# Four graph layers on one Trainium2 core: column-split count matmuls, a last layer in two float16 parts, and neighbour codes stored as byte pairs

## The chip, the cores and the metric

The kernel runs as one program on one core of a Trainium2 chip. The metric is the device time of one execution in microseconds (us); lower is better.

## The reference

`x` is 4096 x 64 and `adj` is 4096 x 4096, sparse, symmetric in where it is non-zero. Each layer normalizes `x`, applies a ReLU and adds the layer's result to `x`.

```python
h = jnp.maximum(_layernorm(x), 0.0); x = x + relu((adj @ h) @ W0.T + b0)              # layer 0
h = jnp.maximum(_layernorm(x), 0.0); x = x + lorentz_attention(h, adj)                # layer 1
h = jnp.maximum(_layernorm(x), 0.0); x = x + expmap0((w @ logmap(h_i, h_j)) @ W2 + b2)# layer 2
h = jnp.maximum(_layernorm(x), 0.0)                                                   # layer 3:
support = h @ W3
mask = (adj != 0)
rank = jnp.cumsum(mask, axis=1); deg = rank[:, -1:]
k = jnp.minimum(deg, 100.0)
pos = rank - (deg - k)
w = mask * jnp.where(pos > 0, 0.5 ** (k - pos), 0.0)
x = x + w @ support + b3
```

A weight of layer 3 is thus a power of two whose exponent is the number of neighbours that follow in the row.

## The kernel before, in words

Five instruction streams (SyncE issues loads, TensorE, VectorE, ScalarE, GpSimd) run in orders written out by hand and meet at semaphores. Node features lie as 32 tiles (T) of 128 nodes by 64 columns.

**Layer 0** takes 64 steps (2 halves of the output nodes x 32 tiles, from the last tile to the first). A step loads a 128 x 2048 tile of the transposed matrix into a ring of eight. VectorE makes its 0/1 mask in bfloat16 (`mask0`, L1543; a ring of four) and adds the tile to the running degree sums (`degree0`, L1549). TensorE (`tile0`) multiplies the tile by the features (4 matmuls of 64 columns, float32, two records each in the trace) and then, in `counts`, the mask by two constant 128 x 128 triangles, `tri_rest` for the tile before and `tri_above` for this one: 8 matmuls of 128 weight columns and 512 moving columns. They accumulate in PSUM the exponent of each weight of layer 3. ScalarE (`make_code`, L1102) turns the 128 x 2048 counts into bytes in two calls, `made[:, k, u * UNIT:(u + 1) * UNIT]`, and stores them in DRAM. `mask0` of step s waits for the counts of step s-3; `counts` waits for the mask and for the codes of the step before. After the last step VectorE copies the sums (`sums_out0_v`, L1472), TensorE applies the weights (`to_nodes`, L580) and VectorE updates X (`update0`, L1515).

**Layers 1 and 2** read the matrix twice more. Layer 1's step has 16 matmuls of 64 columns in float16 (`scores`, L746) and 4 in float32 (`gather1`).

**Layer 3** takes 64 steps again (`step3`). Its tiles come in three groups (GROUPS: tiles 0-7, 8-15, 16-31), because their features are ready in that order: steps 0-15, 16-31 and 32-63. For each step SyncE loads one 128 x 2048 code tile (a ring of 16), and `power(q)` turns code into weight by multiplying it by 128 and writing it as a 16-bit integer, whose bits are the bfloat16 power of two: ScalarE does columns 0-1023 (L1390) and VectorE columns 1024-2047 (L2042). Sixteen weight tiles can wait; `power(q)` for q >= 16 waits for step q-16. TensorE multiplies them by the features, which are cut into three bfloat16 parts (`S3`): 12 matmuls a step. Between the steps the streams carry the end of layer 2 and the features of layer 3 for groups 1 and 2 (`last_passage3`). For group 2 that is: `nodes2(2)` (TensorE, L969) at q 3, `tangent_...` (VectorE, L1883 on) at q 10, `to_tangent(2)` (L888) at q 8 and `weighted(2)` (L898) at q 10 of TensorE, `z_out`, `v_square` (ScalarE, L1055), `length` to `feats3` (VectorE, L1903 to L1963, q 20 to 26) with two roots and a square on ScalarE, `to_last(2)` and `weighted_last(2)` (TensorE, q 25 and 27), then `part_a`, `rest_a`, `part_b`, `rest_b` (L1055, L2148, L1055, L1972), which cut the parts; only then may step 32 start. GpSimd adds the bias to X (L558) once the last parts are made. After step 63 the sums are copied out, turned (L580) and added to X (L2165).

Of the kernel before, what the change touches and what calls it, by code (L numbers as in the profile page):

```python
# [15 lines left out]
I16 = mybir.dt.int16  # L16
ALU = mybir.AluOpType
# [4 lines left out]
D = 64  # L22
P = 128
# [111 lines left out]
W_SCALE = 2.0 ** (127 - MAX_NEIGH)  # L135


def graph_layers(nc, x, adj_t, codes, w0_t, b0, w1_t, b1, wq_t, bq, wk_t, bk, scalars, w2, b2, w3, b3, out):
    ctx = ExitStack()
    with ctx:  # L140
# [46 lines left out]
        trest = sb("trest", [P, TG])  # L187
        tri_above = sb("tri_above", [P, P], BF16)
# [111 lines left out]
        def S3(a, b, k):  # L300
            at = a // TG * HALF
            v = TB[:, at:at + 3 * HALF // 4].bitcast(BF16).rearrange("p (t s c) -> p t s c", t=TG, s=3)
            return v[:, a % TG:a % TG + b - a, k, :]

# [40 lines left out]
        def _(sp):  # L345
# [83 lines left out]
            for q in range(2 * T):  # L429
# [5 lines left out]
                if q >= CODES:  # L435
                    sp.wait_ge(sem("pw_ready_a"), q - CODES + 1)
                    sp.wait_ge(sem("pw_ready_v"), q - CODES + 1)
# [9 lines left out]
        def _(pool):  # L447
# [106 lines left out]
            for g in range(G):  # L554

                pool.wait_ge(sem("parts3_ready"), len(GROUPS))
# [6 lines left out]
        def _(pe):  # L563
# [236 lines left out]
            for s in range(2 * T):  # L800
# [7 lines left out]
                if s == 13:  # L808
                    pe.wait_ge(sem("qhh_out"), 2)
                    fold_low(1, 2)  # L810
                if s == 2 * T - 1:
                    break
# [101 lines left out]
            def weighted_last(q):  # L914
                pe.wait_ge(sem("turned_out"), 2 * q + 2)
                through(q, wbd["w3"][:, :], None)
# [134 lines left out]
        def _(act):  # L1051
# [45 lines left out]
            def make_code(h, s, k, at, stored):  # L1097
                for u in range(2):
# [3 lines left out]
                    nc.scalar.activation(made[:, k, u * UNIT:(u + 1) * UNIT], PS[:, (4 + 2 * u) * BANK:(6 + 2 * u) * BANK],  # L1102
# [179 lines left out]
            def z_out(q, k, scale=1.0, last=False):  # L1282
                one("z_out", part(cen, q), linear_out(q, last), ACT.Copy, ("through", k), scale=scale)
# [9 lines left out]

            def part_b(q):
                one("part_b", S3(*GROUPS[q], 1), part(cen, q), ACT.Copy, ("rest_a", q + 1))
# [8 lines left out]
            def last_passage2(n):  # L1304
# [15 lines left out]
                if n == 53:  # L1320
                    z_out(0, 2, W_SCALE)
                    part_a(0, 2)
                if n == 54:
                    part_b(0)
# [20 lines left out]
            def last_passage3(q):  # L1345
# [8 lines left out]
                if q == 10:  # L1354
                    z_out(1, 4, W_SCALE, True)
                    part_a(1, 4)
                if q == 12:
                    part_b(1)
# [13 lines left out]
                if q == 30:  # L1372
                    one("part_a", S3(*GROUPS[2], 0), linear_out(2), ACT.Copy, ("through", 6), scale=W_SCALE)
                if q == 31:
                    part_b(2)
                if q == 56:
                    one("sums_out3_a", TA[:, 0:UNIT], PS[:, 4 * BANK:6 * BANK], ACT.Copy, ("agg3_done", 48))

            def power(q):
# [10 lines left out]
                nc.scalar.activation(pw(q)[:, 0:UNIT].bitcast(I16), code(q)[:, 0:UNIT], ACT.Copy, scale=BF_STEP)\  # L1390
# [5 lines left out]
            one("sums_out3_a", TA[:, UNIT:UNIT + BANK], banks(6, 7), ACT.Copy, ("agg3_done", 2 * T))  # L1396
# [3 lines left out]
        def _(dve):  # L1400
# [422 lines left out]
            for s in range(2 * T):  # L1823
# [12 lines left out]
                if s == 14:  # L1836
                    copy_out("qll_out_v", q_ll[:, HALF:N], banks(2, 4).bitcast(F16), ("qll_ready", 2))
                if s >= T:
# [127 lines left out]
            def rest_a(q):  # L1966
                dve.wait_ge(sem("part_a"), q + 1)
                V.tensor_tensor(part(cen, q), part(cen, q), S3(*GROUPS[q], 0), ALU.subtract).then_inc(sem("rest_a"), 1)

            def rest_b(q):  # L1970
                dve.wait_ge(sem("part_b"), q + 1)
# [231 lines left out]
```

## Time and profile before

| | us |
|---|---|
| median of 3 runs (1071.85 to 1075.57) | 1072.16 |
| the profiled execution | 1072.81 |
| its span, first to last instruction | 1071.1 |

The span is what the trace shows; 1.7 us of the profiled execution lie around it. Busy shares of the span: TensorE 95%, VectorE 81%, ScalarE 72%, GpSimd 24%. Rows that are merged stretch from their first start to their last end; the idle time in brackets is named with what ended it. A matmul's time overlaps the next one's, so the cost of a block is read from start to start.

### The profile page before, as it was taken

Reading aid. Unit: us, or ns where it says so; the run is one execution under the profiler, and the core shown is the slowest. Engines: PE = TensorE matmul, PEld = TensorE weight load, DVE = VectorE, ACT = ScalarE, POOL = GpSimd, SP = SyncE. Lnnn points to the kernel's source line nnn. Section 1 sums busy time; section 2 is a strip of 40 time slices with the busy share of each in tenths; the row PEclk is TensorE's granted clock in tenths of the full one; section 3 lists DMA queues with packets and bytes.
Section 4 is the critical chain, followed back from the end, with each engine's and each line's share of the span. In section 5 each row is a group of like instructions: output and inputs, shape, how many; then the busy total and the mean of one; then the engine's idle time right before and its main releaser. Section 6 shows DMA issues by size and latency. Waiting matters only on the chain.

```text
span 1071.1 us, 15810 instructions
## 1 busy us (share of the span) xinstructions
PE 1019.4 (95%) x5903; PEld 466.1 (44%) x5922; DVE 865.8 (81%) x1012; ACT 769.7 (72%) x808; POOL 251.7 (24%) x140
## 2 busy tenths in 40 slices
PE   6999999999799999999979998999999998989998
PEld 1333333336644444335434443444544554436544
DVE  6999989997677766797679977787789887897781
ACT  4555545554577666786798899888888889997682
POOL 1079000000001000012035554443334334430010
PEclk9999999999989999999989999999999999999999
DMA  9989998992058899788745336556545535446441
GB/s 329 418 319 423 377 352 296 343 396 97 1 184 285 291 307 309 244 281 275 253 141 183 123 114 197 183 171 195 159 158 187 166 119 177 138 158 205 140 168 40
DMA packets 96346, 238.39 MB, mean 223 GB/s; under 512 B 16400, under 2 KB 45072, under 8 KB 79888
## 3 DMA queue, kind: packets, MB, share of 16 engines
q1 hardware_dynamic: 87056, 220.62, 60.4%
q10 hardware_dynamic: 9216, 16.78, 4.1%
q8 instruction: 47, 0.77, 0.3%
q14 instruction: 27, 0.22, 0.1%
HBM read 219.55 MB, written 17.83 MB: 222 GB/s over the span
## 4 chain that ended last, share of the span: by engine, by line
PE 73%; DVE 11%; ACT 9%; issue 5%; POOL 1%; DMA 1%; SPq 0%; DVEq 0%; ACTq 0%; POOLq 0%
PE PS L568 50%; PE PS L746 9%; PE PS L882 4%; PE PS L851 4%; DVE work L2059 2%; ACT work L1252 2%; ACT work L1260 2%; DVE work L2047 2%; DVE ring L2065 1%; ACT work L1263 1%; DVE work L2053 1%; DVE work L1719 1%; PE PS L580 1%; PE PS L602 1%; ACT work L1246 1%
## 5 line engine op out<-in xcount | busy, mean ns | idle before, releaser
L1102 ACT ACTIVATE work<-PS 128x1024 uint8<-128x1024 f32 x128 | 124.0, 1021 | 106.9 <-PE PS L568 105.1
L1719 DVE TENSOR_TENSOR work<-work,ring 128x1024 f32<-128x1024 f32 x128 | 153.0, 1235 | 59.1 <-ACT work L1177 58.9
L1177 ACT ACTIVATE work<-PS,att_sc 128x1024 f32<-128x1024 f32 x128 | 148.1, 1202 | 68.1 <-PE PS L746 59.1
L568 PE MATMUL PS<-ring,work 128*65 128x256 f32 (+1 forms) x600 | 190.6, 465 | 3.8 <-DVE work L2086 3.8
L546 POOL TENSOR_TENSOR ring<-work,ring 128x1024 f32<-128x1024 f32 x57 | 135.3, 2375 | 232.2 <-DVE work L2059 232.2
L568 PE MATMUL PS<-work 128*64 128x512 f32 (+2 forms) x800 | 151.4, 519 | 1.4 <-ACT work L1246 1.2
L2053 DVE SCALAR_TENSOR_TENSOR work<-PS,work 128x1024 f32<-128x1024 f32 x72 | 88.1, 1223 | 55.1 <-PE PS L568 46.6
L746 PE MATMUL PS<-work 128*64 128x512 f16 x1024 | 124.0, 385 | 3.0 <-ACT work L1177 1.6
L568 PEld LDWEIGHTS PS<-ring,work 128*65 128x65 f32 x600 | 80.6, 138 | 90.8 <-issue 65.5
L1252 ACT ACTIVATE work<-work 128x1024 f32<-128x1024 f32 x72 | 76.0, 1055 | 34.2 <-DVE work L2047 34.1
L746 PEld LDWEIGHTS PS<-work 128*64 128x64 f16 x1024 | 59.0, 111 | 79.4 <-issue 34.7
L2059 DVE SCALAR_TENSOR_TENSOR work<-work 128x1024 f32<-128x1024 f32 x72 | 87.9, 1221 | 2.7 <-ACT work L1267 2.1
L568 PEld LDWEIGHTS PS<-work 128*64 128x64 f32 (+2 forms) x800 | 42.8, 120 | 106.9 <-issue 83.8
L1267 ACT ACTIVATE work<-work 128x1024 f32<-128x1024 f32 x72 | 75.9, 1054 | 9.5 <-DVE work L2053 7.1
L851 PE MATMUL PS<-TB,TA 64*128 64x512 f32 x288 | 81.3, 641 | 1.3 <-DVE work L2053 1.3
L568 PE MATMUL PS<-work,TB 128*64 128x512 bf16 x672 | 76.4, 384 | 2.1 <-DVE work L2042 2.1
L1260 ACT ACTIVATE work<-work 128x1024 f32<-128x1024 f32 x72 | 76.2, 1058 | 2.3
L882 PE MATMUL PS<-ident,work 128*128 128x128 f32 x448 | 62.0, 282 | 14.5 <-DVE work L2059 13.6
L1263 ACT ACTIVATE work<-work 128x1024 f32<-128x1024 f32 x72 | 75.1, 1043 | 0.0
L1549 DVE TENSOR_TENSOR TB<-TB,work 128x2048 f32<-128x2048 f32 x32 | 74.9, 2339 | 0.1
L1246 ACT ACTIVATE work<-PS 128x1024 f32<-128x1024 f32 x72 | 72.6, 1009 | 2.3 <-PE PS L568 2.2
L568 PE MATMUL PS<-work,tri_above 128*128 128x512 bf16 x247 | 73.9, 379 | 0.4
(269 smaller groups left out, 1409.9 us busy)
## 6 DMA issues: line engine op xcount, KB each, us to landing
ring<-in_adj_t SPq DMA_DIRECT2D x96, 1024.0 KB, 5.4
ring<-in_adj_t SPq DMA_DIRECT2D x104, 512.0 KB, 4.1
work<-in_adj_t SPq DMA_DIRECT2D x32, 1024.0 KB, 8.1
codes<-work ACTq DMA_DIRECT2D x64, 256.0 KB, 7.1
ring<-codes SPq DMA_DIRECT2D x64, 256.0 KB, 3.8
H<-in_adj_t SPq DMA_DIRECT2D x24, 512.0 KB, 4.3
X<-in_x SPq DMA_DIRECT2D x2, 256.0 KB, 5.3
X<-in_x SPq DMA_DIRECT2D x1, 512.0 KB, 10.7
```

Source lines behind the costliest of these rows:

```text
L546: nc.gpsimd.tensor_tensor(near(n), sums(n), near(n), ALU.mult).then_inc(sem("near_ready"), 1)
L568: return mm(out_ap, lhsT, rhs, start=starts, stop=True, skip_group_check=True)
L746: ins = mm(o[half_rows(e), :], k_hl[:, jt * P + e * D:jt * P + (e + 1) * D], qs[:, i0:i0 + BANK], start=first, stop=not first)
L851: mm(z_banks(n)[:, q * BANK:(q + 1) * BANK], TA[half_rows(q), p * P:(p + 1) * P], TB[half_rows(q), S * STRIP:(S + 1) * STRIP], start=True, ...
L882: ins = nc.tensor.transpose(PS[:, c:c + P], sums(n)[:, q * BANK + i * P:q * BANK + (i + 1) * P], ident[:, :])
L1102: nc.scalar.activation(made[:, k, u * UNIT:(u + 1) * UNIT], PS[:, (4 + 2 * u) * BANK:(6 + 2 * u) * BANK], ACT.Relu).then_inc(sem("codes_ma ...
L1177: nc.scalar.activation(att[:, u, :], PS[:, (4 + 2 * u) * BANK:(6 + 2 * u) * BANK], ACT.Sigmoid, bias=att_sc[:, 2:3], scale=att_sc[:, 1:2]) ...
L1252: nc.scalar.activation(lnr[:, n % ROT, :], root[:, n % ROT, :], ACT.Ln).then_inc(sem("lnr_ready"), 1)
L1260: nc.scalar.activation(sums(n), lnr[:, n % ROT, :], ACT.Exp, scale=0.5).then_inc(sem("root_ready"), 1)
L1719: V.tensor_tensor(prob[:, m % 4, :], att[:, u, :], ring[:, s % RING, u * UNIT:(u + 1) * UNIT], ALU.mult)\
L2053: V.scalar_tensor_tensor(sums(n), z_banks(n), 1.0, sums(n), ALU.max, ALU.add)\
L2059: V.scalar_tensor_tensor(sums(n), sums(n), TAU_MAX, lnr[:, n % ROT, :], ALU.min, ALU.mult)\
```

## The change

1. `counts`: each matmul of 128 weight columns becomes two of 64, into the two halves of PSUM's rows, over the same mask.
2. Layer 3's features are cut into two float16 parts and not three bfloat16 ones: 8 matmuls a step, `part_b` and `rest_b` are gone. To fit float16's range W3 is scaled by a power of two, found in layer 1 (one 128 x 128 matmul after step 18, seven small VectorE operations after steps 16 and 20), and taken out at the end: three VectorE operations of the tail become one with that factor, and the copies carry a constant scale.
3. The bytes of columns n and 1024+n are stored beside each other (`made[:, k, u:HALF:2]`). ScalarE's `power` reads 352 pairs (704 bytes, at stride 2). VectorE reads the other 672 pairs as 16-bit words and makes two tiles of weights from them: the low byte with AND and shift left, the high byte with shift right and AND.
4. GpSimd's bias addition waits for VectorE's last `power` and not for the last parts. VectorE's addition of the first half moves from q 62 to behind its last `power`.

```diff
@@ pairs of two parts
-            v = TB[:, at:at + 3 * HALF // 4].bitcast(BF16).rearrange("p (t s c) -> p t s c", t=TG, s=3)
+            v = TB[:, at:at + HALF // 2].bitcast(F16).rearrange("p (t s c) -> p t s c", t=TG, s=2)
@@ gpsimd
-                pool.wait_ge(sem("parts3_ready"), len(GROUPS))
+                pool.wait_ge(sem("pw_ready_v"), 4 * T)
@@ counts
                 for c in range(2):
-                    ins = add(PS[:, (4 + 2 * u + c) * BANK:(5 + 2 * u + c) * BANK], lhsT,
-                              mask[:, k, u * UNIT + c * BANK:u * UNIT + (c + 1) * BANK], starts)
+                    for e in range(2):
+                        ins = add(PS[half_rows(e), (4 + 2 * u + c) * BANK:(5 + 2 * u + c) * BANK], lhsT[:, e * D:(e + 1) * D],
+                                  mask[:, k, u * UNIT + c * BANK:u * UNIT + (c + 1) * BANK], starts)
@@ step3
+                pe.wait_ge(sem("pw_ready_a"), q + 1)
                 for u in range(2):
-                    pe.wait_ge(sem("pw_ready_v" if u else "pw_ready_a"), q + 1)
+                    pe.wait_ge(sem("pw_ready_v"), 2 * q + u + 1)
                     b = 4 + 2 * h + u
-                    for n in range(3):
+                    for n in range(2):
@@ make_code
-                    nc.scalar.activation(made[:, k, u * UNIT:(u + 1) * UNIT], PS[:, (4 + 2 * u) * BANK:(6 + 2 * u) * BANK],
+                    nc.scalar.activation(made[:, k, u:HALF:2], PS[:, (4 + 2 * u) * BANK:(6 + 2 * u) * BANK],
                                          ACT.Relu).then_inc(sem("codes_made"), 1)
@@ scalar power
-                nc.scalar.activation(pw(q)[:, 0:UNIT].bitcast(I16), code(q)[:, 0:UNIT], ACT.Copy, scale=BF_STEP)\
+                both = pw(q).bitcast(I16).rearrange("p (u n) -> p u n", u=2)[:, :, 0:POW_A]
+                nc.scalar.activation(both, code(q).rearrange("p (n u) -> p u n", u=2)[:, :, 0:POW_A], ACT.Copy, scale=BF_STEP)\
                   .then_inc(sem("pw_ready_a"), 1)
@@ vector, layer 1
+                if s == 16:
+                    V.scalar_tensor_tensor(w3_abs, wbd["w3"][:, :], -1.0, wbd["w3"][:, :], ALU.mult, ALU.max)\
+                     .then_inc(sem("w3_done"), 1)
+                if s == 20:
+                    dve.wait_ge(sem("w3_summed"), 1)
+                    link(V.tensor_reduce(w3_top[:, :], PS[:, 2 * BANK:2 * BANK + P], AX.X, ALU.max))
...
@@ vector power
-                V.tensor_scalar(pw(q)[:, UNIT:2 * UNIT].bitcast(I16), code(q)[:, UNIT:2 * UNIT], BF_STEP, None, ALU.mult)\
+                two = code(q).bitcast(U16)[:, POW_A:UNIT]
+                V.tensor_scalar(pw(q)[:, POW_A:UNIT].bitcast(U16), two, 0xFF, BF_SHIFT, ALU.bitwise_and, ALU.logical_shift_left)\
                  .then_inc(sem("pw_ready_v"), 1)
+                V.tensor_scalar(pw(q)[:, UNIT + POW_A:2 * UNIT].bitcast(U16), two, 1, 0xFF << BF_SHIFT, ALU.logical_shift_right,
+                                ALU.bitwise_and).then_inc(sem("pw_ready_v"), 1)
@@ vector last_passage3
                 if q == 29:
                     dve.wait_ge(sem("part_a"), 3)
-                    V.scalar_tensor_tensor(part(cen, 2), linear_out(2), W_SCALE, S3(*GROUPS[2], 0), ALU.mult, ALU.subtract)\
-                     .then_inc(sem("rest_a"), 1)
-                if q == 31:
-                    rest_b(2)
+                    V.tensor_tensor(S3(*GROUPS[2], 1), linear_out(2), S3(*GROUPS[2], 0), ALU.subtract)\
+                     .then_inc(sem("parts3_ready"), 1)
```

## Rows read from the trace of the kernel before

**Rows 1.** Window of layer 0: busy PE, PEld, DVE, ACT, POOL; clock, DMA share, GB/s
```profile
50.00:250.00 200.00, 197.46 (x854) 65.15 (x870) 193.03 (x123) 106.41 (x113) 43.97 (x8) 1.00 0.94 353
```

**Rows 2.** Timeline of TensorE, one step of layer 0
```profile
190.59 1.94 PE L568 MATMUL PS<-work,H 128*64 128x512 f32 x8
192.46 0.60 PE L568 MATMUL PS<-work,tri_rest 128*128 128x512 bf16 x2
...
194.29 1.94 PE L568 MATMUL PS<-ring,H 128*64 128x512 f32 x8
```

**Rows 3.** Timeline of TensorE, steps of layer 1
```profile
348.89 1.89 PE L568 MATMUL PS<-work 128*64 128x512 f32 x8
350.61 1.90 PE L746 MATMUL PS<-work 128*64 128x512 f16 x16
352.34 1.89 PE L568 MATMUL PS<-work 128*64 128x512 f32 x8
```

**Rows 4.** Timeline of VectorE in layer 0: one step, and the end
```profile
65.19 1.22 DVE L1543 TENSOR_SCALAR work<-work 128x2048 bf16<-128x2048 f32 x1
...
68.53 1.22 DVE L1543 TENSOR_SCALAR work<-ring 128x2048 bf16<-128x2048 f32 x1
...
245.95 4.62 DVE L1549 TENSOR_TENSOR TB<-TB,work 128x2048 f32<-128x2048 f32 x2
251.77 1.23 DVE L1472 COPY TA<-PS 128x1024 f32<-128x1024 f32 x1 [1.20 <-PE PS L568]
```

**Rows 5.** Timeline of TensorE: where `to_nodes` begins after layer 0
```profile
254.27 0.38 PE L586 MATMUL PS<-brow,bones 96*128 96x512 bf16 x1
```

**Rows 6.** Groups by line and form: busy us, mean ns, idle us before
```profile
L568 PEld LDWEIGHTS PS<-work,TB 128*64 128x64 bf16 x672 | 37.3, 111 | 38.4 <-DVE work L2042 3.1 <-issue 2.4 <-ACT work L1390 0.8
L1102 ACT ACTIVATE work<-PS 128x1024 uint8<-128x1024 f32 x128 | 124.0, 1021 | 106.9 <-PE PS L568 105.1 <-remote 1.8
L1390 ACT ACTIVATE work<-ring 128x1024 int16<-128x1024 uint8 x56 | 54.6, 1044 | 0.0
L1055 ACT ACTIVATE work<-work 128x512 f32<-128x512 f32 x6 | 3.7, 623 | 3.4 <-DVE work L1483 3.2
L1472 DVE COPY work<-PS 128x1024 bf16<-128x1024 bf16 x2 | 1.4, 685 | 0.0
```

**Rows 7.** Timeline of TensorE in layer 3
```profile
964.59 3.79 PE L969 MATMUL PS<-ident,work 65*128 65x65 f32 x32
...
978.40 1.09 PE L888 MATMUL PS<-ident,work 128*128 128x128 f32 x8
...
1005.76 1.09 PE L888 MATMUL PS<-ident,work 128*128 128x128 f32 x8 [1.69 <-DVE work L1963]
...
1019.65 1.49 PE L568 MATMUL PS<-work,TB 128*64 128x512 bf16 x12 [0.86 <-DVE work L2042]
...
1046.50 2.05 PE L580 MATMUL PS<-ident,TA 128*128 128x128 f32 x16
```

**Rows 8.** Timelines of VectorE and GpSimd in layer 3
```profile
975.07 1.22 DVE L1899 TENSOR_TENSOR work<-work 128x1024 f32<-128x1024 f32 x1
...
986.71 1.22 DVE L1903 TENSOR_REDUCE st<-work 128x16 f32<-128x1024 f32 x1 [1.10 <-ACT work L1055]
...
989.64 0.69 DVE L2042 TENSOR_SCALAR work<-ring 128x1024 int16<-128x1024 uint8 x1
990.85 0.18 DVE L1909 TENSOR_TENSOR st<-st 128x16 f32<-128x16 f32 x1 [0.52 <-ACT st L1302]
...
1016.30 5.52 POOL L558 TENSOR_TENSOR X<-X,bias 128x1024 f32<-128x1024 f32 x2 [59.86 <-DVE TB L1972]
```

**Rows 9.** Timeline of VectorE at the end
```profile
1064.26 0.69 DVE L1472 COPY TA<-PS 128x512 f32<-128x512 f32 x1 [13.24 <-PE PS L568]
```

**Rows 10.** Windows, columns as in the first group: a clock that fell
```profile
550.00:555.00 5.00, 2.29 (x10) 0.95 (x11) 3.45 (x4) 4.97 (x6) 0.83 (x2) 0.74 0.68 215
555.00:560.00 5.00, 5.00 (x14) 2.31 (x14) 4.08 (x7) 3.83 (x5) 1.94 (x1) 0.58 0.00 0
```

More of the change, by code:

```diff
@@ L16 @@
 I16 = mybir.dt.int16
+I32 = mybir.dt.int32
+U16 = mybir.dt.uint16
 ALU = mybir.AluOpType
@@ L810, in _ @@
                     fold_low(1, 2)
+                if s == 18:
+                    pe.wait_ge(sem("qll_out_v"), 1)
+                    pe.wait_ge(sem("w3_done"), 1)
+                    mm(PS[:, 2 * BANK:2 * BANK + P], bones[:, :], w3_abs, start=True, stop=True).then_inc(sem("w3_summed"), 1)
                 if s == 2 * T - 1:
@@ L1280, in turned_out, with z_out @@
                 one("turned_out", TA[:, a * D:b * D], PS[:, bank * BANK:bank * BANK + (b - a) * D], ACT.Copy, ("turned", k))
-            def z_out(q, k, scale=1.0, last=False):
-                one("z_out", part(cen, q), linear_out(q, last), ACT.Copy, ("through", k), scale=scale)
+            def z_out(q, k, last=False):
+                one("z_out", part(cen, q), linear_out(q, last), ACT.Copy, ("through", k))
             def v_square(q, k):
@@ L1354, in last_passage3 @@
                 if q == 10:
-                    z_out(1, 4, W_SCALE, True)
+                    z_out(1, 4, last=True)
                     part_a(1, 4)
-                if q == 12:
-                    part_b(1)
                 if q == 13:
@@ L1372, in last_passage3 @@
                 if q == 30:
-                    one("part_a", S3(*GROUPS[2], 0), linear_out(2), ACT.Copy, ("through", 6), scale=W_SCALE)
-                if q == 31:
-                    part_b(2)
+                    one("part_a", S3(*GROUPS[2], 0), linear_out(2), ACT.Copy, ("through", 6))
                 if q == 56:
-                    one("sums_out3_a", TA[:, 0:UNIT], PS[:, 4 * BANK:6 * BANK], ACT.Copy, ("agg3_done", 48))
+                    one("sums_out3_a", TA[:, 0:UNIT], PS[:, 4 * BANK:6 * BANK], ACT.Copy, ("agg3_done", 48),
+                        scale=W_SCALE / (F16_TOP / LN_TOP))
             def power(q):
@@ L1395, in _ @@
                 power(q)
-            one("sums_out3_a", TA[:, UNIT:UNIT + BANK], banks(6, 7), ACT.Copy, ("agg3_done", 2 * T))
+            one("sums_out3_a", TA[:, UNIT:UNIT + BANK], banks(6, 7), ACT.Copy, ("agg3_done", 2 * T),
+                scale=W_SCALE / (F16_TOP / LN_TOP))
         @block.vector
@@ L2159, in _ @@
                 power(q)
-            copy_out("sums_out3_v", TA[:, UNIT + BANK:2 * UNIT], banks(7, 8), ("agg3_done", 2 * T))
+            dve.wait_ge(sem("agg3_nodes"), 1)
+            dve.wait_ge(sem("bias3_added"), 1)
+            V.scalar_tensor_tensor(grp(X, 0), z_of(0, 0), w3_top[:, 0:1], grp(X, 0), ALU.mult, ALU.add)\
+             .then_inc(sem("result_ready"), 1)
+            dve.wait_ge(sem("agg3_done"), 2 * T)
+            V.tensor_scalar(TA[:, UNIT + BANK:2 * UNIT], banks(7, 8), W_SCALE / (F16_TOP / LN_TOP), None, ALU.mult)\
+             .then_inc(sem("sums_out3_v"), 1)
             dve.wait_ge(sem("bias3_added"), G)
```

46 lines of the change are left out of this document (22 added, 24 removed).

## The prediction

> **What bounds the kernel now.** First the windows of layer 0, then its timelines on TensorE and VectorE, then the timelines of layer 3, with the groups by form for the prices. Between 50 and 250 us TensorE is busy 197.5 of 200 us and VectorE 193.0 [rows 1]: two engines are nearly full, and a gain on the first is worth only what the second leaves. A TensorE step is 3.70 us: 1.87 us of float32 matmuls and 1.83 us of counts [rows 2]. VectorE needs 3.34 us for mask and degrees where it doesn't wait [rows 4]. But it also carries other work here, so its idle time from 50 to 250 us is only 200 - 193.03 = 6.97 us [rows 1]. Layer 1's step is, bar the weights, the new layer-0 step: eight float32 records in 1.72 us and sixteen 64-column ones in 1.73 us, 3.45 in all [rows 3].
>
> In layer 3 the last twelve steps run from the end of the turning at 1046.50 + 2.05 = 1048.55 to 1064.26: 15.7 / 12 = 1.31 us for a step of 12 matmuls [rows 7, 9]. ScalarE's share of a step is 1044 ns [rows 6] and VectorE's 0.69 us [rows 8], each about 0.1 us less from start to start, so TensorE bounds the steps that are ready. Up to step 32, though, the bound is the chain that makes group 2's features: from 964.59 (nodes out of layer 2) to the turn at 1005.76, before which TensorE already stands idle for 1.69 us, and on to step 32 at 1019.65 [rows 7].
>
> **Layer 0.** The counts' streaming doesn't shrink, since two 64-column matmuls run side by side. What goes is the time lost at each change between 128 and 64 columns: 3.70 - 3.45 = 0.25 us a step. 64 steps would give 16.0 us. The Trainium skill, TensorEngine Tiling, Key Properties, says that changing the tiling mode drains TensorE; the 0.25 us of rows 2 against rows 3 agree, and the sum goes by the rows. I don't take 16.0 us, because VectorE's work stays. Its last degree addition ends at 245.95 + 4.62 = 250.57 [rows 4]. With TensorE ahead its 6.97 us of idle time [rows 1] vanish: 243.6. Then it copies the sums, 1.23 us less 0.1 of overlap: 244.75. `to_nodes`, at 254.27 before [rows 5], starts right after, at 244.85: **9.4 us** gained. TensorE by itself would be there at 254.3 - 16 = 238.3, so it now waits for masks. Bounds: 0, if the loss isn't one of columns, and 16.
>
> ScalarE's code calls, 2 x 1021 ns a step, had 106.9 us of idle time before them [rows 6]; I cost the byte stride at nothing, as a call goes element by element. No row has such a stride. The loads follow VectorE's releases; at 1.31 MB (tile and codes) per 3.34 us the demand is 392 GB/s, against 353 GB/s at a DMA share of 0.94 now [rows 1]. This is close, and I take it as hidden by the ring of eight. The Trainium skill, TensorEngine Tiling, Restrictions, says that column tiling switches fast weight load off. A 64-column load takes 111 ns [rows 6]; sixteen are 1.8 us of a step, beside the matmuls as in layer 1, whose 3.45 us contain as many. So the rule costs nothing here.
>
> The W3 scaling is one matmul and seven VectorE operations in layer 1; at most 0.4 us for TensorE (a 512-column step of rows 3 is 0.22), and in VectorE's idle time there, it is rounded away below.
>
> **The price of the new `power`.** ScalarE: 704 elements; between 623 ns for 512 and 1044 ns for 1024 [rows 6] that is 781 ns, 0.69 from start to start. VectorE: two operations on 672 16-bit words. A small operation of 16 elements takes 0.18 us [rows 8]. The byte-to-int16 call does 1024 elements in 0.69 us [rows 8], about two per ns behind that fixed part; a 1024-element float32 copy from PSUM takes 1.23 us [rows 4], one per ns, and the same copy in bfloat16 685 ns [rows 6]. So two doublings are seen apart: one for a single SBUF source (with 8-bit or 32-bit elements), one for 16-bit elements where the first isn't available. Both together give 0.17 + 672/4 ns = 0.34 us, 0.26 from start to start, **0.51 us a step**. One alone gives 0.84, none 1.54. I take both, since neither row shows a reason against the other, and keep 0.84 and 1.54 as cases. By the table of perf modes in the Trainium skill, VectorE: DVE Perf Modes, a 16-bit `tensor_scalar` in SBUF does four elements a cycle. That would be about 0.34 us too; no row here shows that speed, nor the bitwise operations. TensorE: 8 of 12 matmuls, **0.87 us**. That float16 weights against a bfloat16 moving side cost what either does alone is taken from rows 3 and 7, where both kinds run at 0.22 us a pair.
>
> **Layer 3, stations of group 2's chain.** (a) The nodes at 964.59 wait for VectorE's sum, which stands behind powers 1 to 3; these are 0.1 us cheaper each, the wait takes over from two shorter steps: -0.5 us. (b) The tangent sum ends at 976.29 [rows 8] and now at 975.8; TensorE, five steps ahead of the old pace, waits for it instead of coming at 978.40 [rows 7]: -2.5. (c) Two steps stand between the turn and `weighted(2)`: -0.9, so `length` begins at 986.71 - 3.4 = 983.3 [rows 8]. VectorE has rest and ten powers before that, 0.7 + 5.1 us from 975.8: ready at 981.6. (d) From `length` to the features 19.0 us. In it, power 20 and the wait for ScalarE's root behind four powers (0.25 us cheaper each) go from 1.25 us (989.64 to 990.85) to about 0.6, powers 21 and 22 give 0.1 each, the second root 0.3: -1.2. Features at 1005.7 - 4.6 = 1001.1. (e) Then turn 1.1, two steps 1.7, weights 2.05 (sixteen matmuls of the kind at 1046.50), `part_a` 1.04, the one difference left 1.2 (as any 1024 elements that read PSUM): 1008.2. Steps 27 and 28 are done by then, step 29 waits for power 29, which stands behind that difference (0.5), and steps 29 to 31 take 2.6. Step 32 starts at 1011.3 and not at 1019.65: **8.3 us**. (f) From 1019.65 to 1064.26 were 44.6 us: 32 steps, 2.05 for turning, and stalls while GpSimd's bias addition slowed VectorE. New: 32 x 0.87 + 2.05 = 29.9: **14.7 us**. ScalarE (0.69) and VectorE (0.51) keep ahead. (g) The late bias starts when VectorE's last power is done, sixteen steps (14 us) before the end, and needs two additions, 5.5 us [rows 8]; without that cover that is what it would cost. The tail of 6.8 us after 1064.26 stays.
>
> Against this stands the clock. Before its features come, TensorE has steps 22 to 24 (2.6 us) in the 8 us from 993, as those powers sit in VectorE's chain. Elsewhere in the trace 2.29 busy us of 5 stand beside clocks of 0.74 and then 0.58: 2.6 and 4.2 us, 6.8 in all, were granted at 1.2 GHz and not 2.4 [rows 10]. If the same happens here and half of it falls where TensorE is in the chain, that costs 3.4 / 2 = **1.7 us**; I count it, with 0 and 3.4 as bounds.
>
> **Sum.** 9.4 + 8.3 + 14.7 - 1.7 = 30.7. The profiled execution took 1072.81 us, so 1042.1; the median of the runs lies 0.65 lower, and I say 1042.
>
> **Rivals.**
> *VectorE at half the hoped speed (0.84 us a step).* Ten powers now end 1.7 us after `length` could start; powers 20 to 25 and 29 add 2.3; the last 32 steps still go at 0.87. Time 1046. For: no 16-bit SBUF call is in the trace. Against: the two doublings.
> *Slower: VectorE at single speed (1.54 us).* It delays the tangents by 4.2 us, `length` by 8.7 more, the features by 6.2 more and the rest by 1; then powers 29 to 63 take 35 x 1.54 = 53.9 us from 1027, to 1081, +0.9 +6.8 = 1088.9, +1.7, less layer 0's 9.4: 1081. It decides alone; the kernel turns slower from about 1.4 us a step. For: two chained bitwise operations appear nowhere. Against: the byte call at L2042 also scales and converts, and is doubled.
> *Layer 0 gains nothing*, because the loss is one of changing between float32 and bfloat16 and not of columns. 1042 + 9.4 = 1051. Against: layer 1 changes between float32 and float16 at no cost.
> *The byte stride makes ScalarE's code calls take twice as long:* 4.1 - 0.2 = 3.9 us a step, 0.2 above the old 3.7, so layer 0 is 13 us longer than before and not 9.4 shorter: 1064. Nothing in the rows speaks for it but that the stride isn't there.
>
> **Chances.** Forecast 0.66 (1038 to 1045: without the clock loss 1040, with it twice 1044), half speed 0.12, nothing in layer 0 0.11, byte stride 0.05, single speed 0.06. The range 1036 to 1052 takes in the first three. A difference under 0.5% (5.4 us) can't be told from none: faster 0.92, same 0.02, slower 0.06.
>
> **What the new profile would show.** Layer 0: TensorE's step at about 3.45 us where no mask is missing, VectorE without idle time and named as what TensorE waited for, `to_nodes` at 245. Layer 3: the operations of `power` on VectorE at 0.34 us, steps at 0.87, idle time of some 3 us before the turn for group 2, a lower clock behind it, GpSimd's addition after the last power. The prediction is wrong if the counts keep their 1.83 us, if the 16-bit operations take over 0.5 us, or if the loads in layer 0 become what VectorE waits for.

## The result and the profile after

The changed kernel takes 1046.24 us (median of 4 runs, 1043.9 to 1049.48) against 1072.01 us (4 runs) for the kernel before: ratio 0.9758, 95% interval 0.9717 to 0.9798, 25.8 us less where 30 were forecast. Its profiled execution took 1044.31 us, 28.5 less than that of before. Where these went is read from four points of the two timelines of TensorE: the second `to_nodes` starts at 250.03 and not at 254.27 [rows 5], 4.2 us gained; the first step of layer 3 starts at 952.91 and not at 958.60, 1.5 us more; and from there to the end of the span are 89.7 us and not 112.5, 22.8 more. Together 28.5. Layer 3 gave more than forecast (21.3), layer 0 less than half (4.2 of 9.4), and the stretch between them 1.5 where nothing was forecast. So the 28.5 lie only 2.2 below the 30.7 of the forecast by some luck: 5.2 are missing in layer 0, and 3.0 came elsewhere.

Windows of the changed kernel, columns as in [rows 1]: layer 0 and three short stretches.

```profile
50.00:250.00 200.00, 189.93 (x1308) 84.59 (x1304) 190.44 (x124) 108.57 (x114) 90.86 (x8) 0.98 0.91 355
150.00:155.00 5.00, 2.98 (x13) 2.76 (x14) 0.00 (x0) 0.00 (x0) 1.74 (x4) 0.54 0.61 253
985.00:990.00 5.00, 2.07 (x18) 0.78 (x14) 4.86 (x7) 0.51 (x1) 0.00 (x0) 1.00 0.38 125
990.00:995.00 5.00, 3.28 (x16) 1.48 (x16) 4.63 (x14) 3.53 (x6) 0.00 (x0) 0.66 0.41 135
```

VectorE was to lose its idle time between 50 and 250 us; it has 9.6 us of it, more than the 7.0 before [rows 1]. GpSimd's busy time has doubled, though its work is the same. The timelines of TensorE, VectorE and GpSimd show why, in that order.

```profile
141.95 1.89 PE L577 MATMUL PS<-work,H 128*64 128x512 f32 x8
143.67 0.60 PE L577 MATMUL PS<-work,tri_rest 128*64 128x512 bf16 x4
...
152.03 0.58 PE L595 MATMUL PS<-brow,bones 96*128 96x512 bf16 x1 [6.46 <-issue]
...
145.05 2.28 DVE L1559 TENSOR_TENSOR TB<-TB,work 128x2048 f32<-128x2048 f32 x1
156.49 1.23 DVE L1525 SCALAR_TENSOR_TENSOR X<-PS,X 128x1024 f32<-128x1024 f32 x1 [9.15 <-PE PS L589]
...
61.06 86.63 POOL L496 CAST bcut<-bias 128x384 bf16<-128x384 f32 x1
147.78 0.91 POOL L498 TENSOR_TENSOR brem<-bias,bcut 128x384 f32<-128x384 f32 x1
148.75 0.50 POOL L500 CAST bcut<-brem 128x384 bf16<-128x384 f32 x1
```

The step has come down as forecast: the f32 matmuls take 1.72 us from start to start, each quarter of the counts 0.43, 3.44 in all. VectorE has no gap up to 147.3. But the pass from the first half to the second needs the bias rows, which GpSimd cuts from the biases. Its first cast has been going on for 86.63 us; it ends at 147.69, 0.4 us after VectorE's last operation. The cast of the same shape at 148.75 takes 0.50 us. TensorE waits 6.5 us for the rows (the view puts it down to "issue", that is to nothing that it shows), VectorE 9.15, and the clock is at its lower level, 1.2 GHz, for nearly all of the 5 us from 150 to 155 (mean 0.54).

Layer 3 on TensorE, then VectorE and GpSimd, then groups by form:

```profile
958.48 3.76 PE L984 MATMUL PS<-ident,work 65*128 65x65 f32 x32 [0.24 <-DVE work L2105]
970.30 1.06 PE L902 MATMUL PS<-ident,work 128*128 128x128 f32 x8
987.62 1.05 PE L577 MATMUL PS<-work,TB 128*64 128x512 bf16 x8 [1.61 <-DVE work L2059]
990.71 3.28 PE L577 MATMUL PS<-work,TB 128*64 128x512 bf16 x16 [2.03 <-DVE work L2059]
995.51 1.09 PE L902 MATMUL PS<-ident,work 128*128 128x128 f32 x8 [1.52 <-DVE work L1985]
1003.13 1.05 PE L577 MATMUL PS<-work,TB 128*64 128x512 bf16 x8 [0.86 <-DVE work L2059]
1005.72 12.28 PE L577 MATMUL PS<-work,TB 128*64 128x512 bf16 x112
1019.53 3.65 PE L577 MATMUL PS<-work,TB 128*64 128x512 bf16 x32
...
977.71 1.22 DVE L1925 TENSOR_REDUCE st<-work 128x16 f32<-128x1024 f32 x1 [2.09 <-ACT work L1071]
1035.69 0.69 DVE L2176 TENSOR_SCALAR TA<-PS 128x512 f32<-128x512 f32 x1 [9.20 <-PE PS L577]
1021.60 4.68 POOL L567 TENSOR_TENSOR X<-X,bias 128x1024 f32<-128x1024 f32 x2 [70.86 <-DVE H L2061]
...
L2059 DVE TENSOR_SCALAR work<-ring 128x672 uint16<-128x672 uint16 x56 | 18.3, 327 | 0.8
L1399 ACT ACTIVATE work<-ring 128x704 int16<-128x704 uint8 x56 | 39.5, 776 | 0.0
L1118 ACT ACTIVATE work<-PS 128x1024 uint8<-128x1024 f32 x128 | 124.2, 1024 | 100.0 <-PE PS L577 99.9
```

Sixteen steps lie between 1005.72 and 1019.53: 0.863 us each. The four idle times from 987 to 1003, 6.0 us together, are all put down to VectorE, which does the last group's features with powers in between.

### The profile page after: what moved, and what is told of

It reads as the page before. It is cut to its first block, busy times and chain, and to the rows that moved or that the text cites. A ratio compares the mean times of both kernels' runs of the same rounds, so it can differ in the third digit from the quotient of the medians.

```text
span 1042.6 us, 16458 instructions
## 1 busy us (share of the span) xinstructions
PE 980.6 (94%) x6171; PEld 475.1 (46%) x6171; DVE 850.0 (82%) x1080; ACT 750.8 (72%) x805; POOL 298.0 (29%) x140
## 4 chain that ended last, share of the span: by engine, by line
PE 62%; DVE 20%; ACT 9%; issue 7%; POOL 1%; DMA 1%; DVEq 0%; SPq 0%; ACTq 0%; POOLq 0%
PE PS L577 39%; PE PS L756 9%; DVE TB L1559 6%; PE PS L896 4%; PE PS L865 4%; DVE work L2078 2%; ACT work L1268 2%; ACT work L1276 2%; DVE work L2066 2%; DVE ring L2084 1%; ACT work L1279 1%; DVE work L2072 1%; PE PS L589 1%; DVE work L1729 1%; ACT work L1262 1%
## 5 line engine op out<-in xcount | busy, mean ns | idle before, releaser
L555 POOL TENSOR_TENSOR ring<-work,ring 128x1024 f32<-128x1024 f32 x57 | 135.3, 2374 | 232.8 <-DVE work L2078 232.7
L1118 ACT ACTIVATE work<-PS 128x1024 uint8<-128x1024 f32 x128 | 124.2, 1024 | 100.0 <-PE PS L577 99.9
L496 POOL CAST bcut<-bias 128x384 bf16<-128x384 f32 x1 | 86.6, 86634 | 0.1
L577 PE MATMUL PS<-work,tri_above 128*64 128x512 bf16 x512 | 77.3, 382 | 0.0
L577 PE MATMUL PS<-work,tri_rest 128*64 128x512 bf16 x496 | 74.6, 379 | 0.0
```

Of the source, the lines that this page charges most:

```text
L555: nc.gpsimd.tensor_tensor(near(n), sums(n), near(n), ALU.mult).then_inc(sem("near_ready"), 1)
L577: return mm(out_ap, lhsT, rhs, start=starts, stop=True, skip_group_check=True)
L1118: nc.scalar.activation(made[:, k, u:HALF:2], PS[:, (4 + 2 * u) * BANK:(6 + 2 * u) * BANK], ACT.Relu).then_inc(sem("codes_made"), 1)
```

## The experiments

Each ratio is against the kernel before, measured on the same chip. For the stages this table is used (us), one traced execution a row, read from the timelines of TensorE: its first matmul of layer 0; from there to the second `to_nodes`, taken at its first matmul with the weights, 0.2 to 0.4 us behind the bias row that the result section reads; the "passage", which is the time from that `to_nodes` to the first one of layer 1 and so holds the end of layer 0 and half of layer 1; from the first step of layer 3 to the end of the span; and the length of GpSimd's first cast of the biases.

| kernel | first matmul | to 2nd `to_nodes` | passage | layer 3 | GpSimd's first cast |
|---|---|---|---|---|---|
| before | 13.45 | 241.0 | 172.0 | 112.5 | 31.3 |
| changed | 13.14 | 237.1 | 170.6 | 89.7 | 86.6 |
| counts of 64 alone | 12.94 | 237.0 | 170.2 | 111.9 | 86.8 |
| `tri_rest` of 64 alone | 12.94 | 255.0 | 173.0 | 111.7 | 8.7 |
| changed, counts of 128 | 11.74 | 239.5 | 170.5 | 91.1 | 52.0 |
| VectorE stops for the bias | 13.59 | 232.7 | 173.1 | 89.7 | 61.7 |
| biases early | 24.50 | 229.4 | 179.0 | 89.7 | none |
| column halves | 13.61 | 237.6 | 171.8 | 100.2 | 86.7 |
| powers twice | 13.24 | 237.1 | 170.6 | 116.4 | 86.6 |
| bias beside | 13.22 | 237.0 | 170.4 | 95.9 | 87.1 |
| early, reordered | 24.43 | 228.9 | 180.8 | 88.8 | none |
| VectorE makes the rows | 13.44 | 230.8 | 174.9 | 91.6 | none |
| pairs alone | 13.82 | 241.0 | 172.0 | 110.7 | 32.0 |
| copy first | 12.72 | 226.6 | 177.1 | 92.6 | none |

**Counts of 64 columns alone.**
```
-  ins = add(PS[:, (4 + 2 * u + c) * BANK:(5 + 2 * u + c) * BANK], lhsT,
+  for e in range(2):
+      ins = add(PS[half_rows(e), (4 + 2 * u + c) * BANK:(5 + 2 * u + c) * BANK], lhsT[:, e * D:(e + 1) * D],
```


> The kernel before with one edit: each count matmul of 128 columns becomes two of 64 columns. Byte pairs, halves and late bias are as before. Theory: the edit alone gives layer 0 what the changed kernel has there, a step of 3.44 us instead of 3.70, and also its stall: GpSimd's cast of the biases stretches to 80 us or more beside a VectorE without pauses, so TensorE waits for the bias rows near 147 us and starts the second `to_nodes` near 250 instead of 244.9. Layer 3 keeps its 105.7 us from its first step to the copy at its end. Sum: 4 to 6 us off, near 1067, ratio 0.995. Rival 1 (the stretched cast comes from something else in the changed kernel): the cast stays near 61 us, `to_nodes` starts at 245, 9 to 11 us off, ratio 0.990. Rival 2 (the pause between the two kinds of count matmul isn't removed by equal shapes alone): step 3.70, no change.


1069.72 us, ratio 0.9959 (0.9936 to 0.9982). The step is 3.44 us, the cast 86.8, layer 3 nearly unchanged: the stall comes with the counts alone, and of the 9.4 us forecast 4 to 5 are left.

**`tri_rest` alone in 64 columns.** The same edit only where `lhsT` is `tri_rest`.


> The kernel before with one edit: of the count matmuls only those with the weights tri_rest are split into two of 64 columns; those with tri_above stay at 128. TensorE's column shape then changes four times in a step instead of twice. Theory (TensorE drains at each change of the column shape, 0.25 us a step for two changes): layer-0 steps of about 3.95 us. Rival (the pause belongs to the change of data type from the float32 matmul to the bfloat16 one, which this edit leaves alone): 3.70 us as before.


1086.79 us in one run. Two records of its steady state:
```profile
192.29 1.94 PE L568 MATMUL PS<-work,H 128*64 128x512 f32 x8
...
196.22 1.94 PE L568 MATMUL PS<-work,H 128*64 128x512 f32 x8
```
3.93 us a step, 0.49 more than with equal columns, where two changes a step cost 0.25. So it is the change of column shape that costs, 0.12 us each time; a change of type is there in the 3.44 us step too, and costs nothing that shows.

This run also tells what ends the cast. GpSimd and VectorE in it:
```profile
59.88 8.65 POOL L487 CAST bcut<-bias 128x384 bf16<-128x384 f32 x1
...
65.89 2.28 DVE L1556 TENSOR_TENSOR TB<-TB,work 128x2048 f32<-128x2048 f32 x1
68.35 1.26 DVE L1550 TENSOR_SCALAR work<-ring 128x2048 bf16<-128x2048 f32 x1 [0.19 <-PE PS L568]
69.53 3.00 DVE L1556 TENSOR_TENSOR TB<-TB,work 128x2048 f32<-128x2048 f32 x1
```
With TensorE slower, VectorE must wait sooner. Its first gap is 0.19 us long and begins at 68.17; the cast ends at 68.53. From then on both engines' operations stretch in turn (3.00 us instead of 2.28).

**The changed kernel with counts of 128 columns.** The first edit undone.


> The changed kernel with the count matmuls at 128 columns again: byte pairs, two halves and late bias alone. Theory: layer 0 is as it was before (step 3.70, second `to_nodes` at 254.3, the bias cast near 61 us, no wait for the bias rows), and layer 3 keeps its whole gain of 22.9 us from its first step to the copy at its end (82.8 instead of 105.7). Sum: 1072.2 - 22.9 = 1049.3, ratio 0.979. Rival (part of layer 3's gain comes with the earlier start of layer 0, through the low clock at its beginning): layer 3 longer than 84 us.


1046.76 us, ratio 0.9734 (0.9692 to 0.9776). By the run times no difference from the changed kernel can be told. In the traces the changed kernel has 2.4 us less up to `to_nodes` and 1.4 less in layer 3; of these, 1.4 are taken back by a later first matmul, and its span is 2.7 us shorter in all. From the first step of layer 3 to the copy at its end are 84.2 us, not the 82.8 of the theory and just over the rival's mark of 84. The low clock may be the reason (0.78 and 0.54 from 960 to 970, against 0.78 and 0.88 in the changed kernel); that isn't shown. The cast again ends with VectorE's first gap:
```profile
59.06 51.97 POOL L496 CAST bcut<-bias 128x384 bf16<-128x384 f32 x1
...
110.89 1.23 DVE L1552 TENSOR_SCALAR work<-work 128x2048 bf16<-128x2048 f32 x1 [0.22 <-PE PS L577]
```

**VectorE stops for the bias rows.**
```
 if h:
+    dve.wait_ge(sem("brow_ready"), 3)
```


> The changed kernel with a wait more: VectorE waits for the three bias rows of GpSimd before it starts the second half of layer 0. It has nothing else to do there than run ahead. Theory (GpSimd's cast is held up by VectorE's unbroken work and moves on as soon as VectorE stops): the cast ends about 1 us after VectorE's last mask of the first half, the five pieces behind it take 4 us, TensorE's wait in the passage shrinks from 9 us of VectorE's idle time to about 4.5, the second `to_nodes` starts near 246, and the run is about 4 us shorter than the changed kernel: near 1040, ratio 0.972. Rival (the cast is simply a long piece of work, 87 us, whatever VectorE does): it ends at 147.7 again, and the added wait makes VectorE start later than now, 1 to 3 us slower than the changed kernel.


1042.56 us, ratio 0.9701 (0.9659 to 0.9743). VectorE ends its first half at 122.1:
```profile
60.76 61.72 POOL L496 CAST bcut<-bias 128x384 bf16<-128x384 f32 x1
...
126.75 1.23 DVE L1553 TENSOR_SCALAR work<-ring 128x2048 bf16<-128x2048 f32 x1 [4.64 <-POOL brow L505]
```
The cast ends at 122.48. With a wait of 4.64 us put in `to_nodes` comes 4.4 us earlier than in the changed kernel, and the passage gives 2.5 of them back (173.1 against 170.6). By the run times the two can't be told apart: the intervals overlap (the changed kernel's is 0.9717 to 0.9798). In the four kernels read so far (`tri_rest` alone, counts of 128, this one and the changed kernel) VectorE's gaps begin at 68.17, 110.67, 122.11 and 147.33 and the cast ends at 68.53, 111.03, 122.48 and 147.69: 0.36 us later each time, whatever else differs. So the cause of the stall is shown: VectorE's unbroken work keeps GpSimd out.

In the kernel before the cast ends at 92.34, although VectorE's first gap that the trace shows begins at 124.98. TensorE, VectorE and GpSimd there:
```profile
91.79 1.94 PE L568 MATMUL PS<-work,H 128*64 128x512 f32 x8
...
89.69 2.29 DVE L1549 TENSOR_TENSOR TB<-TB,work 128x2048 f32<-128x2048 f32 x1
91.90 1.52 DVE L1543 TENSOR_SCALAR work<-work 128x2048 bf16<-128x2048 f32 x1
...
61.05 31.29 POOL L487 CAST bcut<-bias 128x384 bf16<-128x384 f32 x1
```
The addition ends at 91.98, and the cast again 0.36 us later. The mask at 91.90 starts 0.11 us behind TensorE's next step (91.79), as the one at 110.89 does in the run before this (110.78); the mask ahead of it still started 0.46 us behind (88.55 and 88.09). So it seems to be the first mask that had to wait for TensorE's counts, for too short a time to leave a gap in the trace. With pairs alone, below, it is the same (92.22 behind 92.10, the cast up to 92.67). This is read from the traces; no run tests it.

**Biases loaded first, cut by VectorE.** The loads go to the head of ScalarE's queue, the seven operations to the head of VectorE's, none to GpSimd.


> The changed kernel with the biases loaded first, on ScalarE's queue, and cut into their three bfloat16 parts by VectorE before the nodes have landed; GpSimd does none of it. Theory (the wait for the bias rows is all that took layer 0's gain): no idle time at the passage between the halves beyond the 1 to 2 us of before, the second `to_nodes` at about 245, layer 3 unchanged, 5 us off the changed kernel: near 1039, ratio 0.971. Rival (something else waits there next, such as the masks' own chain or TensorE's clock after the passage): `to_nodes` later than 247, less than 3 us off.


1056.02 us, ratio 0.9834 (0.9801 to 0.9866): a miss. The theory's part holds (229.4 us to `to_nodes`, 7.7 less), but the edit has two prices.
```profile
16.40 0.36 DVE L1497 CAST bcut<-bias 128x384 bf16<-128x384 f32 x1 [16.40 <-DMA bias<-in_b]
24.50 3.68 PE L554 MATMUL PS<-ring,H 128*64 128x512 f32 x8 [14.87 <-DVE H L1493]
...
270.00:275.00 5.00, 5.00 (x22) 3.80 (x21) 0.90 (x5) 0.00 (x0) 0.00 (x0) 0.50 0.00 0
```
VectorE, with the features of the first nodes behind these seven operations, waits for the biases till 16.40, and TensorE starts 11.4 us late. And the passage takes 8.4 us more, with the clock at 1.2 GHz for long stretches; the rival had named the clock there.

**Column halves and not byte pairs.** Stored codes and `power` as before: ScalarE converts 1024 columns, VectorE the other 1024.


> The changed kernel without the byte pairs: codes stored one to a byte in the order of before, ScalarE makes the powers of one half of each tile by a conversion of 1,024 elements and VectorE those of the other half, as before. The two float16 halves, the late bias and the 64-column counts stay. Theory (TensorE at 0.86 us a step is only the bound because the pairs took work from ScalarE): ScalarE sets the step at 0.94 us, the same as its 945 ns for one conversion of before, about 0.08 x 30 steps late in layer 3 = 2.5 us, and its catching up after each passage costs 1 to 2 more: near 1048, ratio 0.978. Rival 1 (the halves alone bring all of it, the steps wait for TensorE's or the features' chain): 1044, no difference. Rival 2 (each engine falls further behind in the first half of the layer, where both also do the features): 8 us or more.


1057.13 us, ratio 0.9854 (0.9828 to 0.9879). My theory fell; layer 3 is 10.5 us longer, as the second rival has it (8 or more), though not chiefly in the first half of the layer. ScalarE's power takes 0.95 us from start to start, TensorE's step 0.86, so ScalarE is behind when it has to copy the sums out at tile 56:
```profile
1025.95 7.67 ACT L1398 ACTIVATE work<-ring 128x1024 int16<-128x1024 uint8 x8
1033.53 1.00 ACT L1071 ACTIVATE TA<-PS 128x1024 f32<-128x1024 f32 x1
...
1034.58 2.83 PE L589 MATMUL PS<-ident,TA 128*128 128x128 f32 x16 [3.51 <-ACT TA L1071]
```
That wait is 3.5 us; 2.0 lie in the first steps of the layer, where this run's clock was lower (0.50 from 965 to 970) and which may be chance; the rest is spread over the middle, part of it at the lower clock (0.50 and 0.51 from 995 to 1005, and 0.66 from 1035 to 1040, behind the wait).

**Pairs alone.** The kernel before with byte pairs, three bfloat16 parts, early bias, 128-column counts.


> The kernel before with byte pairs alone: codes stored and taken apart as in the changed kernel, but three bfloat16 parts of the features, the early bias and the 128-column counts of before. Theory (TensorE sets the steps of layer 3 at 1.29 us with three parts, whatever the powers cost): layer 0 as before, the second `to_nodes` at 254.5; layer 3 gains only where VectorE's chain in the middle is shortened by 0.1 to 0.35 us a step over some twenty tiles and ScalarE catches up sooner after its copies: 1 to 5 us, ratio 0.995 to 0.999. Rival (the pairs carry half of the gain by themselves): 10 us off, ratio 0.990.


1074.35 us, ratio 1.0022 (0.9997 to 1.0048): no change, and 1.8 us in layer 3 by the trace. So pairs alone 1.8, halves with the late bias alone 12.3 (14.3 without the lower clock at its start), both 22.8: by these traces 6.7 to 8.7 us come from the two together. The steps say why: pairs alone leave TensorE's step of 12 matmuls as the bound, and halves alone leave ScalarE's 0.95 us.

**Powers twice.** Both of VectorE's operations are done twice from tile 4 on.


> The changed kernel with both of VectorE's power operations done twice from tile 4 on, chained, so that VectorE spends about 1.0 to 1.2 us a step on powers instead of 0.49. The output is the same. It stands for the rivals in which VectorE's new operations run at half or single speed. Theory: VectorE becomes the bound of layer 3 with about 1.1 us a step against TensorE's 0.86, plus its features' work between: 0.25 x 60 = 15 us at most, of which the gaps in which TensorE waits for the features anyway take up 5: 8 to 12 us longer than the changed kernel, 1052 to 1056. Rival (the passage of the features sets the layer's length, the steps behind it are slack): under 4 us longer.


1070.6 us in one run, more than either theory said. One of its last steps, as they all are there:
```profile
1017.75 1.05 PE L577 MATMUL PS<-H,TB 128*64 128x512 bf16 x8 [0.17 <-DVE H L2063]
```
VectorE needs 1.23 us a step and sets it. That is all of the gain but 2 us; from this one run I estimate that the kernel would have broken even at about 1.25 us a step on VectorE. The twofold operations are chained by waits, so this stands for a slow VectorE and not for slow operations exactly.

**The late bias undone.**
```
-  pool.wait_ge(sem("pw_ready_v"), 4 * T)
+  pool.wait_ge(sem("parts3_ready"), len(GROUPS))
```


> The changed kernel with GpSimd's two additions of the last bias as early as before, as soon as the third group's features stand, beside VectorE's powers, instead of behind them. Theory (GpSimd and VectorE slow each other): the additions take over 4 us each instead of 2.36, VectorE's power operations beside them go from 0.33 us to 0.5 or more, and TensorE waits up to 2 us for powers there as far as VectorE isn't some tiles ahead: 0 to 2 us more from the first step of the layer to the end (89.7 us in the changed kernel). Rival (they don't touch each other here): 2.36 us each, 0.33 us an operation, 89.7 us.


1051.74 us in one run; layer 3 is 6.2 us longer. GpSimd, VectorE and TensorE:
```profile
1004.94 4.77 POOL L567 TENSOR_TENSOR X<-X,bias 128x1024 f32<-128x1024 f32 x2 [54.30 <-DVE TB L2165]
...
1005.02 2.49 DVE L2061 TENSOR_SCALAR work<-ring 128x672 uint16<-128x672 uint16 x1
1007.43 2.48 DVE L2059 TENSOR_SCALAR H<-ring 128x672 uint16<-128x672 uint16 x1
...
1007.56 0.62 PE L577 MATMUL PS<-work,TB 128*64 128x512 bf16 x4 [1.69 <-DVE work L2061]
1010.05 3.29 PE L577 MATMUL PS<-H,TB 128*64 128x512 bf16 x16 [1.86 <-DVE H L2059]
```
Each addition holds one operation of VectorE for its whole length: 2.49 us instead of 0.33. The additions themselves aren't slowed. TensorE loses 3.6 us to it, and its clock falls behind the waits (sixteen matmuls took 3.29 us, where 1.92 is usual): 5.0 of the 6.2 us. The rest lies ahead of the additions, where the clock was lower than in the changed kernel (0.58 from 995 to 1000, against 1.00), and may be chance.

**Early biases and another order in layer 3.** On VectorE the pieces of tiles 20 to 22, from `length` on, stand at tile 23 and so behind powers 20 to 22, and the rest at tile 32; ScalarE's root stands at tile 17. The pieces of tiles 23 to 26 stayed where they were, so the edit is less than what was announced.


> The kernel with the early biases and, on top, another order of VectorE's and ScalarE's work in layer 3: VectorE makes the powers of tiles 20 to 22 before it starts on the length of the last group, the later passages of that group stand three tiles further on, and ScalarE takes the root at tile 17 instead of 19. Theory (TensorE waits 1.6 and 0.9 us at 988 and 1003 because VectorE does the features' chain while the next powers are due): these waits go, the layer is 2 to 2.5 us shorter: near 1037, ratio 0.968. Rival (the chain of the features is what the end waits for, and a later start of it moves its end): the second wait grows by what the first loses, no change against the early biases alone.


1050.14 us, ratio 0.9801 (0.9773 to 0.983), not told apart from the early biases alone. Layer 3 is 88.8 us: 0.9 gained and not 2 to 2.5.
```profile
1003.07 1.92 PE L554 MATMUL PS<-work,TB 128*64 128x512 bf16 x16 [2.37 <-DVE work L2048]
1007.88 1.67 PE L879 MATMUL PS<-ident,work 128*128 128x128 f32 x8 [2.89 <-DVE work L1974]
```
What the steps no longer wait, the turn of the features waits: the rival, all but the 0.9.

**VectorE makes the rows between the halves.** The seven operations stand at the head of VectorE's second half; in layer 3 ScalarE takes 480 pairs and not 352 in tiles 21 to 28, and the rest comes at tile 32.


> The changed kernel with three edits. Layer 0: VectorE itself cuts the biases into their three parts and makes the bias rows, about 3 us of work, between its last mask of the first half and its first of the second; GpSimd does none of it. Layer 3: ScalarE takes 480 of each 512 byte pairs in tiles 21 to 28 instead of 352, and VectorE takes the third group's rest at tile 32 instead of 29. Theory for layer 0 (the stretched cast is the whole loss): TensorE passes from step 37 to 38 in 5.9 us as in the kernel that waits for the bias, and its second `to_nodes` starts 230 us after the first step, or a little before, instead of 235.2: 5 us off. Rival: VectorE's 3 us move its second half by as much, 232 or more. Theory for layer 3 (VectorE's chain for the last group, with the powers between, sets the four waits of 6.0 us together): VectorE saves 8 times 0.33 us = 2.6 us of it, ScalarE has 4.8, 2.6 and 2.1 us of idle time for its eight times 0.26 us more; the wait of 0.86 goes: the layer is 2 to 3 us shorter, 87 us from its first step to the end of the run instead of 89.7. Rival (ScalarE's powers become the last ones there): no gain. Sum of both: near 1037, ratio 0.967 to 0.970; 1042 or more if both rivals hold.


1041.59 us, ratio 0.9705 (0.9677 to 0.9733). The layer-0 part came out: `to_nodes` 230.8 us after the first matmul (237.1), and the seven operations took 2.8 us at 121.9. The expectation counts a tile as 512 pairs; it has 1024, so VectorE's operation only fell from 0.245 to 0.21 us from start to start, 0.07 a tile and not 0.33. The layer-3 part so didn't test what it was made for; the turn of the features comes 42.7 us into the layer, as before it (42.6). Layer 3 is 1.9 us longer than in the changed kernel, behind that turn, with the clock at 0.51 from 995 to 1000 (1.00 in the changed kernel). And 4.3 us of layer 0's gain were given back in the passage, at the lower clock:
```profile
243.86 0.61 PE L580 MATMUL PS<-brow,bones 96*128 96x512 bf16 x1 [3.89 <-DVE TA L1467]
...
240.00:250.00 10.00, 6.14 (x30) 5.71 (x31) 5.39 (x5) 1.09 (x2) 0.00 (x0) 0.66 0.07 26
```

**Copy first.** VectorE makes the rows between the halves as in the run above, layer 3 is that of the changed kernel, and VectorE copies the sums out ahead of its last two additions:
```
+copy_out("sums_out0_v", TA[:, UNIT:2 * UNIT], PS[:, UNIT:2 * UNIT], ("agg0_done", 2 * T))
 for k in (RING0 - 2, RING0 - 1):
     degree0(1, 2 * T - RING0 + k, k)
-copy_out("sums_out0_v", TA[:, UNIT:2 * UNIT], PS[:, UNIT:2 * UNIT], ("agg0_done", 2 * T))
```


> The changed kernel with two edits in layer 0 and none in layer 3: VectorE makes the bias rows between the halves (as in the run before, 2.8 us of work there), and it copies the sums of the second half out before its last two degree additions instead of behind them. Theory (VectorE's order at the end of layer 0 makes TensorE wait 3.9 us for the copy, and the half clock from 244 to 250 and again behind it follows on that wait): the copy starts at 238 us, as soon as VectorE has done the third-last addition, the second `to_nodes` starts 224 us after the first step instead of 228.2 (235.2 in the changed kernel) without idle time ahead of it, the two additions (4.4 us) lie beside it, and the passage to the next `to_nodes` takes 170.5 us at full clock instead of 174.9. Sum: 11 us off the changed kernel less 1 for a later first step: near 1034, ratio 0.965. Rival (the additions are needed at once, by the next pieces of the passage): the wait comes back ahead of the degrees' matmuls, 4 us off the changed kernel, 1040. Rival 2 (the clock falls in the passage whatever the wait): 174 us again, near 1037.


1038.9 us (1034.15 to 1042.77), ratio 0.9668 (0.9637 to 0.9699): the lowest ratio, its interval clear of the changed kernel's but not of those where VectorE stops for the rows or makes them. The wait is gone (`to_nodes` follows the turning at once, 226.6 us after the first matmul), and the second rival is right all the same, by more than it said:
```profile
238.18 1.09 PE L581 MATMUL PS<-ident,work 128*128 128x128 f32 x8
239.11 0.38 PE L575 MATMUL PS<-brow,bones 96*128 96x512 bf16 x1
...
250.00:260.00 10.00, 10.00 (x45) 8.53 (x46) 5.43 (x20) 1.36 (x3) 0.00 (x0) 0.51 0.00 1
```
The clock was at 1.2 GHz from 250 to 260, although TensorE had no idle time there nor in the 25 us before, and the passage took 177.1 us. Layer 3, with the same code as in the changed kernel, took 92.5 us and not 89.7, with 10.2 us at the lower clock between 985 and 1000 where the changed kernel has 3.4.

## Why the prediction was right, and where not

*Layer 0, 9.4 us: the step of the argument that failed.* The loss at each change of column shape (0.25 us a step) and the bound by VectorE were right. The step "with TensorE ahead its 6.97 us of idle time vanish" put what follows from it at nothing: GpSimd gets in only when VectorE first has to wait for TensorE. Its cast took 31 us before and 87 after, and 5 of the 9.4 us went into TensorE's wait for the bias rows. By the run times the 64-column counts can't be told from those of 128 in the changed kernel (0.9758 and 0.9734). With that wait removed and the order of VectorE kept, 10.2 us are gained up to `to_nodes`. The Trainium skill, SBUF — State Buffer, Who interferes with whom, says that a VectorE operation in a two-port mode and a GpSimd operation exclude each other, that the one issued first has the shared ports for the whole instruction, and that a VectorE operation with two SBUF inputs contends with a GpSimd operation that reads SBUF. The 2.49 us of VectorE's operation beside the bias addition agree. That a row of such operations without a gap keeps GpSimd out for 86 us the page doesn't say; the casts show it.

*Passage, 0 forecast, 1.4 us gained:* 10.2 us at the lower clock and not 13.6 between 240 and 320 us.

*Layer 3.* Counted from its first step: the nodes 0.4 us earlier (0.5 forecast), the turn 2.4 (2.5), `length` 3.3 (3.4), the features' turn 4.56 (4.6). VectorE's operation 0.327 us (0.34), ScalarE's 776 ns (781), a step 0.863 (0.87). In (e) I took 1019.65 for the start of step 32; it is its second half, and the step began at 1017.98. So (e) gave 6.6 us and (f) 16.3, together 22.9 as against 23.0. The term that was off is the clock's 1.7 us. The clock was at its lower level for 3.4 us, from 990.1 to 993.5, and made two steps take 3.28 us and not 1.92 (the row at 990.71). But TensorE then waited 1.52 us for the features all the same, so the 1.4 us came out of that wait. The waits were named right, before the turn (forecast some 3 us; 1.5 there and 3.6 in the steps ahead of it).

*The late bias* was costed as hidden, 5.5 us without cover. Undone it costs 6.2, though not for the additions themselves but for the powers that they stop.

*The rivals.* Half and single speed are out by 0.327 us an operation. The price of slow VectorE operations was set too low: break-even lies at about 1.25 us a step and not at 1.4. That the loss in layer 0 belongs to the change of type is out by the 3.93 us step. The byte stride costs 3 ns a call (1024 against 1021 [rows 6]).

What stays open: what makes the clock fall in the passage with TensorE fully busy. It falls within one block, in which matmuls of 128x1 alternate with single ones of 128x512: with copy first (0.50 from 250 to 255), and with `tri_rest` alone (0.50 from 280 to 285, no idle time in the 25 us before). In the kernel before the same block ran at 1.00 (260 to 268). It wasn't taken apart.

## What to carry to other kernels

Before a change that lets an engine run without gaps, look at who works in the gaps: here GpSimd's small preparation stood far ahead of its need and became the critical wait, and 2.8 us of the same work on VectorE cost less than 87 us on an engine that gets no turn. Two changes that each relieve another engine are to be priced together: by their traces 1.8 and 12.3 to 14.3 us alone were 22.8 together. A gain ahead of a passage with pauses can be partly returned there by the clock, so read it behind the passage and not ahead of it.

## What the hardware showed unexpectedly

- GpSimd's cast of 128x384 took 8.7, 52.0, 61.7 and 86.6 us, each time until 0.36 us behind the start of VectorE's first gap, which need be no longer than 0.2 us; and 31.3 us in the kernel before, until the first mask that, as it seems, had to wait for TensorE. The second cast of that shape took 0.50 us with VectorE idle and 2.45 where the two engines took turns.
- The other way round, an addition of 128x1024 on GpSimd (2.4 us) stopped VectorE's 0.33 us operation for 2.2 us.
- The passage goes with the time at the lower clock between 240 and 320 us (from the windows, (1 - clock) x 2 x length): 10.2 us and 170.6; 13.6 and 172.0; 17.0 and 174.9; 17.1 and 173.1; 20.4 and 177.1; 23.9 and 179.0; 27.3 and 180.8 (early, reordered). The same work thus took up to 10.2 us more, and 6.5 us of what the copy-first kernel gained ahead of it were returned so.
- Chained bitwise operations on 16-bit words in SBUF took 0.327 us for 672 elements (0.245 from start to start), where the forecast's two doublings together gave 0.34 and either alone 0.42 from start to start; and float16 weights against a bfloat16 moving side ran at the speed of equal types (0.863 us for eight matmuls).
